# GNN stack on one core: node product moved ahead of the roots, means' product moved back, first edge residual in its own bank, transfer queue in order of readiness

## The reference, cut to what matters

```
x1 = layernorm(x + relu([x, max over edges (x[dst] - x[src])] @ W0 + b0))
x  = silu(x1 @ lin_W.T + lin_b)
f1, f2 = (two products of the edge attributes)
h1 = silu((segment_sum(f1 * x[src]) @ rel1 + rel1_b + x @ root1) @ lin1_W.T + lin1_b)   # h2 alike with f2
h  = concat(h1, h2) @ cat_W.T + cat_b + x
for i in range(3): h = silu(h @ lins_W[i].T + lins_b[i]) + h
```

## Time and profile before

| | |
|---|---|
| median of 3 runs | 5421.13 us (5409.99 to 5424.0) |
| profiled execution, its own time | 5410.58 us |
| its span | 5408.9 us |
| busy: PE, DVE, POOL, ACT | 78%, 79%, 75%, 67% |
| `nodes01`, loop part | about 200 to 1840 us, 18.64 us per pair of steps |
| `edges1` | about 1919 to 3060 us; 10.97 us per step from 2149 us on |

### The profile page before, as it was taken

One profiled execution on the slowest core, in us unless ns is written; L12 is line 12 of the kernel. 1 busy time (PEld: TensorE's weight loads), 2 busy tenths in 40 slices (PEclk: granted clock), 3 DMA queues, 4 the chain that ended last, 5 costly groups with the idle time before them and its releaser, 6 DMA issues. The chain is left out here.

```text
span 5408.9 us, 82889 instructions
## 1 busy us (share of the span) xinstructions
PE 4223.2 (78%) x18435; PEld 2618.7 (48%) x18558; DVE 4247.1 (79%) x8746; ACT 3645.5 (67%) x9127; POOL 4062.4 (75%) x4129
## 2 busy tenths in 40 slices
PE   6999999999999978999999888888576745551000
PEld 3555555555555533444444588887454534440000
DVE  7888888888888746788788799999788854457776
ACT  3777777777777635666666688888688854446665
POOL 6788888888888777777777177777777767777777
PEclk9999999999999989999999999999655567665555
DMA  6877787777777646777777699999798967774443
GB/s 181 206 208 205 204 200 205 208 204 199 209 205 203 163 106 202 208 203 205 207 202 207 207 383 376 377 378 374 272 281 280 285 196 227 229 242 152 135 135 104
DMA packets 850458, 1213.29 MB, mean 224 GB/s; under 512 B 347599, under 2 KB 517001, under 8 KB 850215
## 3 DMA queue, kind: packets, MB, share of 16 engines
q1 hardware_dynamic: 744566, 1059.81, 61.4%
q0 software_dynamic: 100352, 149.23, 12.7%
q10 hardware_dynamic: 5296, 1.73, 0.1%
HBM read 648.60 MB, written 438.76 MB: 201 GB/s over the span
## 5 line engine op out<-in xcount | busy, mean ns | idle before, releaser
L847 ACT ACTIVATE p_s<-p_ps,cols 128x512 f32<-128x512 f32 x588 | 404.5, 688 | 341.1 <-PE p_ps L801 216.7
L729 POOL DMA_INDIRECT home<-edge_row_cols,scatter_cols x392 | 447.1, 1141 | 119.3 <-issue 119.3
L198 POOL DMA_INDIRECT out<-u_res,scatter_cols x392 | 407.7, 1040 | 121.7 <-issue 118.4
L1196 POOL DMA_INDIRECT ring_rows<-t_rows,home_cols x384 | 409.1, 1065 | 119.2 <-issue 88.5
L191 POOL DMA_INDIRECT u_rows<-t_rows,home_cols x392 | 388.2, 990 | 145.5 <-issue 117.3
L191 POOL DMA_INDIRECT ring_rows<-t_rows,home_cols x400 | 396.7, 992 | 126.3 <-issue 114.7
L722 POOL DMA_INDIRECT p_xs<-in_x,src_cols x388 | 387.0, 997 | 123.3 <-issue 117.0
L722 POOL DMA_INDIRECT p_xd<-in_x,dst_cols x388 | 398.3, 1027 | 107.2 <-issue 107.2
L1205 POOL DMA_INDIRECT home_cols<-home,src_cols x376 | 368.1, 979 | 144.2 <-issue 86.0
L212 DVE BATCH_NORM_STATS2 r_counts<-r_v 128x6 f32<-128x256 f32 x980 | 373.4, 422 | 11.0 <-issue 0.9
L227 ACT ACTIVATE r_x<-r_v,r_nm,r_rs 128x128 f32<-128x128 f32 x784 | 321.8, 482 | 83.0 <-DVE r_nm L1773 83.0
(11 more groups left out here) (307 smaller groups left out, 13894.1 us busy)
## 6 DMA issues: line engine op xcount, KB each, us to landing
ring_rows<-in_x SPq DMA_DIRECT2D x98, 512.0 KB, 6.2
p_xT<-p_xt SPq DMA_DIRECT2D x392, 128.0 KB
t_rows<-p_o SPq DMA_DIRECT2D x98, 512.0 KB
p_x1T<-p_oT SPq DMA_DIRECT2D x392, 128.0 KB
hT<-ring_own SPq DMA_DIRECT2D x98, 512.0 KB
q_hn<-hT SPq DMA_DIRECT2D x98, 512.0 KB
r_h<-hT SPq DMA_DIRECT2D x98, 512.0 KB
r_x<-t_rows SPq DMA_DIRECT2D x98, 512.0 KB
```

The costliest lines, as they stand in the source:

```text
L198: nc.gpsimd.indirect_dma_start(out=table, out_offset=bass.IndirectOffsetOnAxis(ap=idx[:, j:j + 1], axis=0), in_=rows[:, j, :], in_offset=N ...
L729: nc.gpsimd.indirect_dma_start(out=tab["home"], out_offset=bass.IndirectOffsetOnAxis(ap=s["scat"][:, k:k + 1], axis=0), in_=s["at"][:, k:k ...
L847: nc.scalar.activation(act_out[i][:, :], flat(bank_r if i else bank_t), ACT.Silu, bias=col(LS0 + i)).then_inc(r_act[i], 1)
L1196: nc.gpsimd.indirect_dma_start(out=rows[:, e % 4, j, :], out_offset=None, in_=tab["t1"], in_offset=bass.IndirectOffsetOnAxis(ap=s["home"][ ...
```

## The change

1. `nodes01`, PE: the block's own product (L794) moves from behind the two root products to ahead of them, right behind L779.
2. `nodes01`, DVE: the means' product `nm` (L952) moves from behind L944 to behind the statistics and the second residual sum.
3. `nodes01`, POOL: `homes(3)` moves from ahead of the wait for the stores to behind the eight row gathers.
4. `edges1`, PE and ACT: the first residual product goes to `bank_t` instead of `bank_r` and no longer waits for `r_act[2]`; that wait now stands at the second. One fixed step waits for the mask copies out of `bank_t`.
5. `edges1`, SP: within a step the order becomes store, ends row, swap, [step 0: `home` table], node blocks, own squares and attributes, carry row.

```diff
@@ nodes01, gpsimd
             homes(2)
-            homes(3)
...
                 gather(nc, ring["rows"][:, b], tab["t1"], s["home"][:, b * G:(b + 1) * G], to_edges1["rows_in"][b])
+            homes(3)
@@ nodes01, tensor: behind the matmul into bank_t
+                if t.live(NB):
+                    q = t.pair()
+                    pe.wait_ge(xT_in[q.of(2)], landed(2, q, 4))
+                    after(pe, biased, t.b)
+                    for j in range(G):
+                        i = nc.tensor.matmul(bank_o[:, j, :], xT[:, q.of(2), j, :, :, t.slot % 2].rearrange("p a i -> p (a i)"), first["w0"][:, :],
+                                             start=True, stop=True)
+                    i.then_inc(product, 1)
                 n = t.back(7)
...
-                if t.live(NB):
...  (the same eight lines, behind the roots)
@@ nodes01, vector
-                q = t.pair().back(1)
-                if even and q.live(QB):
...  (the means' product)
@@ behind residual(1, n)
+                q = t.pair().back(1)
+                if even and q.live(QB):
+                    lo, hi = batch(q)
+                    dve.wait_ge(rooted, q.b + 1)
...
@@ edges1, sync
             for t in range(EB + 10):
+                e = t - 6
+                if live(e, EB):
+                    sp.wait_ge(r_added[2], e + 1)
+                    sp.dma_start(tab["eT"][e], hs[3][:, e % 4, :]).then_inc(h_saved[e % 4], DMA)
+                e = t - 3
...  (ends row)
+                if t % 2 == 0 and live(t, EB):
+                    q = t // 2
+                    sp.wait_ge(squared, t + 2)
+                    after(sp, lined_g, t - 2)
+                    swap_groups(sp, xT[:, q % 2], squares[:, q % 2], xT_in[q % 2])
+                if t == 0:
+                    for c in range(NC):
...  (home table, before ahead of the loop)
@@ edges1, tensor
                     pe.wait_ge(r0_ready, n.b + 1)
-                    after(pe, r_act[2], n.b)
-                    nc.tensor.matmul(flat(bank_r), s["lins"][:, 0, :], hs[0][:, n.of(2), :],
+                    if t.fixed and t.b == MASK_AT + 1:
+                        pe.wait_ge(copied, 2)
+                    nc.tensor.matmul(flat(bank_t), s["lins"][:, 0, :], hs[0][:, n.of(2), :],
                                      start=True, stop=True).then_inc(r_done[0], 1)
...
                     pe.wait_ge(r_added[0], n.b + 1)
+                    after(pe, r_act[2], n.b)
@@ edges1, scalar
-                nc.scalar.activation(act_out[i][:, :], flat(bank_r), ACT.Silu, bias=col(LS0 + i)).then_inc(r_act[i], 1)
+                nc.scalar.activation(act_out[i][:, :], flat(bank_r if i else bank_t), ACT.Silu,
+                                     bias=col(LS0 + i)).then_inc(r_act[i], 1)
```

More of the change, by code:

```diff
@@ L962, in step @@
                     residual(1, n)
+                q = t.pair().back(1)
+                if even and q.live(QB):
+                    lo, hi = batch(q)
+                    dve.wait_ge(rooted, q.b + 1)
+                    after(dve, applied, 2 * (q.b - 1), NB)
+                    after(dve, e_applied, q.b - 1 - BEHIND)
+                    nc.vector.scalar_tensor_tensor(nm[:, q.of(2), lo:hi], st[:, q.of(2), lo:hi, MEAN_OF], -1.0,
+                                                   rs[:, q.of(2), lo:hi], ALU.mult, ALU.mult).then_inc(scaled, 1)
                 if not even and e.live(EB):
@@ L1132, in _ @@
             home_v = tab["home"].rearrange("(b p h) o -> p b (h o)", p=P, h=2 * G)
-            for c in range(NC):
-                sp.dma_start(home[:, c].rearrange("p (b h) j -> p b (h j)", h=2),
-                             home_v[:, c * NB // 4:(c + 1) * NB // 4, :]).then_inc(home_in[c], DMA)
             for t in range(EB + 10):
+                e = t - 6
[3 more added lines that the diff above has]
+                e = t - 3
+                if e % 2 == 0 and live(e, EB):
+                    after(sp, masked, e - 2)
+                    load_row_pair(sp, ends[:, e % 4:e % 4 + 2, :], tab["ends"], e // 2, ends_in[e // 2 % 2])
+                if t % 2 == 0 and live(t, EB):
[5 more added lines that the diff above has]
+                    for c in range(NC):
+                        sp.dma_start(home[:, c].rearrange("p (b h) j -> p b (h j)", h=2),
+                                     home_v[:, c * NB // 4:(c + 1) * NB // 4, :]).then_inc(home_in[c], DMA)
                 if t == DENSE_AT:
@@ L1161, in _ @@
                         load_row_pair(sp, cont[:, t % 4:t % 4 + 2, :], tab["cont"], t // 2, cont_in[t // 2 % 2])
[L1162 to L1174, removed]
         @block.gpsimd
```

## The result

The median of six executions is 5365.3 us (5352.4 to 5381.9), that of the kernel before, timed beside it, 5417.5 (5405.8 to 5430.8); the ratio is 0.991, 95% interval 0.988 to 0.993. The forecast was 5369. The profiled execution took 5362.7 us, and its span is 5361.0 us against 5408.9, 48 us less, where the sum said 47.

| stage | before | after | difference | forecast |
|---|---|---|---|---|
| `nodes01`, start to the last guard L1001 | 1892.4 | 1870.4 | -22.0 | -19 |
| last guard to the first turn in `edges1` | 26.7 | 29.8 | +3.1 | +3.5 |
| first turn to the product of the gathered row in step 8 | 112.0 | 111.5 | -0.5 | -1.3 |
| seven catch-up steps (step 9 to 16) | 106.5 | 82.4 | -24.1 | -25 |
| 80 steps (17 to 97) | 10.966 each | 10.954 each | -1.0 | -5 |

What follows compares the result with a forecast made beforehand. PE's stream was taken to bound the node loop, and waits for SP's swap the catch-up steps. Terms -19 + 3.5 - 5 - 25 - 1.3 = -47 took 5410.6 to 5363.8; median forecast 5369 us, range 5345 to 5405.

Steps and rivals of the forecast that it cites:

- part 4: Edge layer 1, own bank for the first residual: 0.06 of 0.25 us left per step, -5 us.
- rival B: Node loop: GpSimd is thrown out of step, more issues meeting DVE operations; +73 us, 5442; chance 0.07.
- Part 1: Node loop, PE: product ahead of the roots removes a 0.18 us stall in both steps, 0.36 per pair.
- Part 2: Node loop, DVE and ACT: late `nm` delays L878 and the odd L779, giving back 0.15 us per pair.
- GpSimd's share: Node loop: GpSimd, 17.6 us per pair without lengthened issues, follows a pair of 18.43 at no cost.
- A: Rival: GpSimd sets the node loop's pace, so the 19 us go: 5388; chance 0.16.
- 1.28 against 0.99: Node loop, GpSimd: an issue with a DVE transpose in its middle against the source gathers' mean, contradicting the skill's list.
- the lock has held for 1600 us: Node loop: argument that GpSimd stays in step with DVE, held against being thrown out of step.
- Part 3: End of node phase, GpSimd: `homes(3)` behind the gathers ends it 2.7 to 3.7 us later, +3.5.
- Part 5: Edge layer 1, SP's order: three waits and half clocks go in catch-up steps, -25 us; at step 0, -1.3.
- C: Rival: catch-up steps gain nothing because another load becomes the late transfer: 5394; chance 0.10.

Runs made afterwards that it cites:

- experiment 1: Changed kernel with `nm` moved back ahead of the statistics and second residual sum: median 5415.5 us, ratio 1.000; its two profiled executions took 5349.1 and 5416.3.
- experiment 6: Changed kernel with 16 node steps per loop round (`UNROLL`) instead of 8: median 5414.8 us.
- experiment 5: Changed kernel with `homes(3)` back ahead of GpSimd's wait for the stores: median 5363.5 us, ratio 0.9909.
- experiment 7: Changed kernel with the product `A1 x run` ahead of `R1 x xx` in `edges1`: 5356.2 us, ratio 0.990.
- experiment 8: Changed kernel with DVE's turn of the gathered rows behind the first residual sum in `edges1`: median 5394.5 us.
- experiment 9: Changed kernel with both `A1 x run` first and DVE's turn behind the first residual sum in `edges1`: median 5393.5 us.
- experiment 11: Changed kernel with `A1 x run` first in `edges1` and `homes(3)` back ahead of GpSimd's wait: 5356.7 us, ratio 0.9896.
- experiment 3: Changed kernel with the block's product back behind the two root products, `nm` left late: 5439.2 us, ratio 1.0042.
- experiment 4: Kernel before with only SP's new order in edge layer 1: 5388.7 us, ratio 0.9958.
- experiment 10: Changed kernel with a memset and a wait behind the third and fourth issue of each GpSimd group in the node phase: 5573.9 us, ratio 1.029.
- experiment 2: Changed kernel with `nm` back and GpSimd's fourth source-row gather left out from the third edge block on: four executions of 5353 to 5382 us.

## Why the prediction was right

Both large terms, the nodes and the catch-up steps, are right in size and in cause. The small term of part 4 is not, and my argument against rival B did not hold.

- **Part 1** was right: 0.37 per pair goes with the two stalls, from 18.643 to 18.27, where I had 0.36. What comes next in line is not PE's.
- **Part 2** found the right wait at the right place, the odd L779 behind L878, with nearly the right mean: 0.12 per pair, where I took 0.15. But I had it in each pair alike. In three of four `nm` starts 5.90 after L779 (my 5.7, counted from L779, is 6.05), and L878 follows L227's start by 1.55, not by the 1.65 of its row: it ends at 8.2 to 8.4 instead of the 8.68 of my sum, and L779 does not wait. In the fourth DVE turns its loop, 0.55 us that lay inside its wait for the product before. The pair of the earlier trace rows waits 0.73 there; the pair with the turn waits 0.18:

```profile
982.30 0.69 DVE L907 TENSOR_TENSOR ring_own<-p_s,p_r 128x512 f32<-128x512 f32 x1 [0.45 <-issue]
...
984.99 0.69 DVE L942 TENSOR_TENSOR p_v<-p_ps,b_row 128x512 f32<-128x512 f32 x1 [0.18 <-PE p_ps L794]
```

  The change took that cover away, and I did not ask what else lay under it. Experiments 1 and 6 show it: with `nm` ahead of two operations no pair is late, and the period goes with the round of the loop.
- **GpSimd's share** came out as taken: it followed from 18.63 to 18.34 with the same instructions, so 18.63 was not its own speed, and A fell. By the rule of the Trainium skill ("SBUF — State Buffer", section "Who interferes with whom") that I had weighed, the transposes and statistics of this loop would not hold GpSimd back, and A would have come true; it did not. Which operations of DVE lengthen an issue no run varied. My 1.28 against 0.99 set a scatter against the mean of the gathers; the scatters' own mean is 1.14. A better sign is in the whole stretch of the earlier trace rows: each of the 256 issues above 1.15 us has a transpose or a statistic starting 0.2 to 0.55 us behind its own start. But 79 with one there are short, and after, 86 gathers take some 1.25 with none near, so the cause is open in part.
- **Rival B** did not happen in this kernel but is real. The same node code with `nm` in its old place is B, by their times, in 11 of 13 executions: +62.7 us between its two profiles, where I had put B at +73, and by the power, not by gathered rows. My "the lock has held for 1600 us" was no argument: the code has two rhythms, and a trace shows one. With `nm` last in its step it starts 5.90 after L779 and needs the power only then; in the old place it starts at 4.1 to 5.1 when nothing holds it. After, the power ends at 3.6, so both places would do. In experiments 5, 7, 8, 9 and 11, with the same node code, it ends at 4.8 and in every fourth pair at 5.3, and `nm` still waits in no pair; experiment 1 shows that in the old place it would have waited. All six traces have pairs of 18.39 on average. The 19 executions of the four kernels among these without a moved turn end at 5381.9 at most; the 17 of experiments 8 and 9 reach 5419 with the same node code, only one of each was profiled, and so a second rhythm of the nodes is not excluded there. So the moved `nm`, measured as a cost of 0.12 per pair, is what keeps the product's gain, by the later place at which the power is needed. No run varied that room alone.
- **Part 3** was right: +3.1 against +3.5, and experiment 5 takes it back to within a tenth. The wait is 3.71, at the upper end of my 2.7 to 3.7.
- **Part 4** was mis-sized: -1.0 instead of -5. The stall for `xx` stayed as said, but not 0.06 per step is left of 0.25, for two reasons. I read one step of the earlier trace rows for all 83, and each fourth took 10.92 before already, so that at most some 3.7 us were there. And the second residual L1241 became late behind DVE, by 0.01 to 0.03 and in each fourth step by 0.09. The step that failed is that I followed PE and ACT past the removed stall, and not DVE. The lateness differs from execution to execution: where it is least (experiments 1, 3 and 5, the same `edges1` code) the steady steps gain 3.0 to 3.5 us.
- **Part 5** was right: -24.1 against -25, and C fell, by a run of its own (experiment 4). At the start the gain was 0.5, not 1.3.
- The rest, -3.4 in code that hardly changed, covered the miss of part 4. That is luck: the same stretch was 2367 to 2395 us long in the profiles of the changed kernel and its variants, 2368.5 after.

The median lies 2.6 us above the profiled execution, which I had put at 5.3; the profiled execution itself took 5362.7 where the sum said 5363.8.

## What to carry to other kernels

Where a stall is taken from an engine that looks fully busy, ask of every other engine what its own wait at that place was covering: loop turns lie under waits, and show up once those go. An engine that fills the whole period without ever waiting can have more than one stable rhythm. An operation that consumes its result stands best as late in its own queue as its reader allows. One profile is not enough to know which rhythm a kernel runs in: look at all its executions, and compare a small difference between two profiles with what the same code does in others. An in-order transfer queue should be sorted by when things are ready; here that was worth half of the gain for nothing.

## What I had not expected of the hardware

- At 8 node steps per round the turn of the loop leaves DVE without an instruction for 0.45 us before and 0.21 after, and what follows starts 0.5 to 0.6 later. At 16 steps it is 3.7 to 5.3 us, PE stands 3.1 to 4.7 us for DVE's sum, and in the pair shown it then runs for 5 us at half its clock (granted 0.50).
- GpSimd's issue of an indirect transfer took 0.94 to 1.49 us in the same program; the twelve of a pair took 12.25 us in one execution of the kernel of experiment 1 and 13.11 in the other.
- In experiment 10 a scatter behind a memset and a wait started 0.81 us after the memset, a gather 0.27.
- All that comes behind `edges1`, the same code in all kernels, took from 2335 to 2363 us from profile to profile. Of the difference 16 us stand in one group of GpSimd: its 392 gathers `u_rows` took 0.99 us each after, and 1.03 in two of the long ones (experiments 2 and 8).
